# Four sums of z per chunk on GpSimd instead of two on VectorE, in the first stage of a three-part layer

## Chip, cores and metric

One Trainium2 chip, one core of it. The metric is the device time of the whole program in microseconds, the median of several executions. The engines are TensorE (matrix products), VectorE, ScalarE, GpSimd, and SyncE, which here only issues DMAs. Their names in the profile: PE is TensorE, PEld its weight loads, DVE VectorE, ACT ScalarE, POOL GpSimd, SP SyncE.

## The reference

```python
# first stage: for 64 rows (batch), T = 128 tokens, N = 64 complex states, L = 1024
Wc = Wc * num * _reciprocal(den * Lam, EPS)
P = dt_Lambda[..., None] * pos - P_max[..., None]
K = jnp.einsum('chn,hnl->chl', Wc, jnp.exp(P))
h = K.real                                  # (64, 128, 1024)
# then, per batch row:
h = h + attention(layernorm(h), Wq, Wk, Wv, Wo)   # 32 heads, 8 kv heads, rope, causal
h = h + ffn(layernorm(h), A, B, Wr, br)           # 8 softly mixed low-rank experts
```

For each token the first stage is a product of a 64 x 128 matrix (real and imaginary parts of the weights) by a 128 x 1024 matrix of complex powers. Only this stage is touched by the change.

## The kernel before, in words

`s4_stage` is the first stage, `layer_stage` (attention and feed-forward, 64 batch rows one after the other) the second. The second starts when all blocks of the first are through.

**Factored powers.** The 1024 positions of a token are taken apart into 4 parts of 256 (`TOPS`), and each part into 16 x 16 (`DIG`, `SEG`). The tile `z` of a *pair* of tokens holds, per token, two halves (s = 0 and 1) of 256 columns: the products of 16 digits by 16 steps. The factor of the part goes into the other operand, `xw`, which is the weight of the token times the power of its part, in real and imaginary form. The matmuls of a token are `hps += xw x z`, once for each half of z, for two column ranges of `hps`. If the two halves are added beforehand (the *sum* of this text), one matmul of a kind does for two. In the profile a matmul of f32 counts as two instructions, so a pair has 16 instructions in L612 without the sum and 8 with it.

**Loops.** 128 tokens are 64 pairs g; a *window* w has 4 tokens (2 pairs), a *chunk* k has 16 tokens, which is 4 windows or 8 pairs; there are 32 windows and 8 chunks. Pair 8k is the first of chunk k. `summed(g)` says which pairs are summed: before, pairs 3 and 7 of each chunk, and all eight pairs of the last chunk.

**The order on each engine**, written out by hand in one program each; they meet only at semaphores:

- VectorE, per window w: `swapped(w + 1)` (L467, L473: writes `pi`, the swapped part of the products, and the fourth token of `xw`; each reads one input from SBUF and one from PSUM), `table_z` for the two pairs (L487; `u` in PSUM, `tab` in SBUF), then the sums (L494; both inputs in `z`, SBUF) if there are any, then an extra step: in the first window of a chunk `angles(k + 1)` (L425 to L435), in the third `tables(k + 1)` (L441, L445), in the fourth `digits(k + 1)` (L454 to L458). At the end of windows 4k+1, 4k+2, 4k+3 comes `weight_lo` (L499) for a piece of the second stage's weights: `wq_lo`, `wo_lo`, `wkv_lo`; `aw_lo` and `bm_lo` come once, in windows 4 and 8. `angles`, `tables`, `digits` and `weight_lo` have all their inputs in SBUF. `table_z(g)` waits for the matmuls of pair g - 4 (four buffers of z), `swapped(w + 1)` for `add(w)`.
- ScalarE, per window w: in the second window of a chunk first the three sines (L351 to L354); then for each of the 4 tokens the products of window w + 3 (L364, four instructions, for 3 of the 4 tokens) and `evict` (L374, the copy of `hps` to `hout`, after the token's matmuls); at the end `weight_hi` (L379) for the piece whose `weight_lo` VectorE has in window w + 1. `weight_lo` waits for it.
- GpSimd, per window w: in windows 4k+1, 4k+3 and 4k+4 first a step of the tables of chunk k+1: `first_angles` (L255), `table_i` (L259), `digits_m1` (L262), each behind a wait for the `weight_lo` that VectorE has in the window before (`w_lo`); then `add(w)` (L322, `xw += pi`), which waits for `swapped(w)`.
- TensorE, per window: waits for `add(w)` (`xw_done`), per pair for `table_z` (`z_made`) and, if the pair is summed, for its sum (`z_sum`); then the matmuls (L612) of the two tokens, each of which waits until `hps` has been copied four tokens earlier.
- SyncE loads `x` and the weights and stores each pair's `hout`.

The condition and the sum as they stand:

```python
def summed(g):
    return g // (TC // 2) == CHUNKS - 1 or g % 2 == 1 and g // 2 % PER_CHUNK in SUM_AT   # SUM_AT = (1, 3)

def sum_z(g):                                                                            # VectorE
    zg = z[g % ZR][:, :, :].rearrange("p (t s) l -> p t s l", s=2)
    dve.wait_ge(z_made, g + 1)
    V.tensor_tensor(zg[:, :, 0, :], zg[:, :, 0, :], zg[:, :, 1, :], ALU.add).then_inc(z_sum, 1)
```

Of the kernel before, what the change touches and what calls it, by code (L numbers as in the profile page):

```python
# [15 lines left out]
ALU = mybir.AluOpType  # L16
# [5 lines left out]
T = 128  # L22
# [24 lines left out]
TC = 16  # L47
CHUNKS = T // TC
WIN = 4
WINDOWS = T // WIN  # L50
PER_CHUNK = TC // WIN
XT = 8
ZR = 4
# [75 lines left out]
def s4_stage(nc, x, log_dt, lam, wq, wk, wv, wo, aw, bm, br, consts, h0, W):  # L129
# [4 lines left out]
    with ExitStack() as ctx:  # L134
        def sb(name, shape, dt=f32):
            return ctx.enter_context(nc.sbuf_tensor(name, shape, dt))

        def sem(name):
            return ctx.enter_context(nc.semaphore(name))
# [7 lines left out]
        z = [sb(f"z{i}", [P, 4, QROW]) for i in range(ZR)]  # L147
# [68 lines left out]
        z_made = sem("z_made")  # L216
        z_sum = sem("z_sum")
# [2 lines left out]
        h_sent = [sem(f"h_sent{i}") for i in range(HR)]  # L220

        TV, TA, TP = 10, 3, 3
        SUM_AT = (1, 3)

        def summed(g):
            return g // (TC // 2) == CHUNKS - 1 or g % 2 == 1 and g // 2 % PER_CHUNK in SUM_AT

        def sums_before(g):
            return sum(summed(n) for n in range(g))
# [24 lines left out]
        def first_angles(eng, k):  # L254
            return eng.tensor_tensor(theta[:, :, :], across(zi, k, NPOS),  # L255
                                     pos[:, :].unsqueeze(1).broadcast_to([P, TC, NPOS]), ALU.mult)

        def table_i(eng, k):
            return eng.tensor_tensor(tab[k % 2][:, :, 1, :], expo[:, k * TC:k * TC + TC, :], theta[:, :, :], ALU.mult)  # L259

        def digits_m1(eng, k):
            return eng.tensor_tensor(dm1[:, :, :].rearrange("p t (s n) -> p t s n", s=2), across(rr, k, 2, DIG),  # L262
                                     tab[k % 2][:, :, :, 0:DIG], ALU.mult)

        with nc.Block() as block:
# [50 lines left out]
            @block.gpsimd  # L316
            def _(pool):
                def add(w):
                    pool.wait_ge(pr_done, w + 1)
                    pool.wait_ge(pi_done, w + 1)  # L320
                    xw_w = xw[w % XWR]
                    nc.gpsimd.tensor_tensor(xw_w[:, :, :, :], xw_w[:, :, :, :], pi[:, :, :, :],  # L322
                                            ALU.add).then_inc(xw_done, 1)

                pool.wait_ge(pre_v, N_PRE)
                for w in range(WINDOWS):
                    k, at = (w - 1) // PER_CHUNK, (w - 1) % PER_CHUNK
                    if w >= 1 and k + 1 < CHUNKS:
                        lows = sum(piece[0] < w - 1 for piece in PIECES)
                        if at in (0, 2, 3) and lows:  # L330
                            pool.wait_ge(w_lo, lows)
                        if at == 0:
                            pool.wait_ge(tab_v, TV * k + 10)
                            first_angles(nc.gpsimd, k + 1).then_inc(tab_p, 1)
                        if at == 2:
                            pool.wait_ge(tab_a, TA * (k + 1) + 2)
                            pool.wait_ge(z_made, k * (TC // 2))
                            table_i(nc.gpsimd, k + 1).then_inc(tab_p, 1)
                        if at == 3:
                            pool.wait_ge(tab_v, TV * (k + 1) + 7)  # L340
                            pool.wait_ge(tab_p, TP * (k + 1) + 2)
                            digits_m1(nc.gpsimd, k + 1).then_inc(tab_p, 1)
                    add(w)

            @block.scalar
            def _(act):
# [29 lines left out]
                def weight_hi(n):  # L376
                    _, name, k, width, _ = PIECES[n]
                    act.wait_ge(w_in[n % 2], loads_until(n))
                    A.activation(weight(name + "_hi", k), wst[n % 2][:, 0:width], ACT.Copy, scale=WS).then_inc(w_hi, 1)  # L379
# [30 lines left out]
            def _(dve):  # L410
                V = nc.vector
# [26 lines left out]
                def tables(k):  # L438
                    dve.wait_ge(tab_a, TA * k + 3)
                    dve.wait_ge(pre_a, 7 if k else 6)  # L440
                    V.tensor_scalar(half[:, :, :], half[:, :, :], -2.0, 1.0, ALU.mult, ALU.add).then_inc(tab_v, 1)  # L441
                    if k == 0:
                        table_i(V, k).then_inc(tab_p, 1)
                    dve.wait_ge(tab_v, TV * k + 6)
                    V.tensor_tensor(tab[k % 2][:, :, 0, :], expo[:, k * TC:k * TC + TC, :], half[:, :, :],  # L445
                                    ALU.mult).then_inc(tab_v, 1)
# [14 lines left out]
                def swapped(w):  # L461
                    q, slot = w // 2, w // 2 % XR
                    dve.wait_ge(x_in[slot], 48 * (q // XR + 1))
                    if w >= 1:
                        dve.wait_ge(xw_done, w)
                    t = WIN * w
                    V.tensor_tensor(pi[:, :, :, :],  # L467
                                    xb[slot][:, t % XT:t % XT + WIN, :].unsqueeze(2).broadcast_to([P, WIN, TOPS, NB]),
                                    top_i3[:, t:t + WIN, :].unsqueeze(3).broadcast_to([P, WIN, TOPS, NB]), ALU.mult)
                    if w >= XWR:  # L470
                        dve.wait_ge(tok_done, WIN * (w - XWR) + WIN)
                    rest, n = slice(t % XT + ON_ACT, t % XT + WIN), WIN - ON_ACT
                    V.tensor_tensor(xw[w % XWR][:, ON_ACT:, :, :],  # L473
                                    xa[slot][:, rest, :].unsqueeze(2).broadcast_to([P, n, TOPS, NB]),
                                    top_p3[:, t + ON_ACT:t + WIN, :].unsqueeze(3).broadcast_to([P, n, TOPS, NB]),
                                    ALU.mult).then_inc(pi_done, 1)

                def table_z(g):
                    k, at = g // (TC // 2), g % (TC // 2)
                    if g >= ZR:  # L480
                        dve.wait_ge(tok_done, 2 * (g - ZR) + 2)
                    if at == 0:
                        dve.wait_ge(tab_v, TV * k + 10)
                        dve.wait_ge(tab_p, TP * k + 2)
                    digit = u[k % 2][:, :].rearrange("p (s n) -> p s n", n=DIG)[:, 4 * at:4 * at + 4, :]
                    step_ = tab[k % 2][:, 2 * at:2 * at + 2, :, DIG:].rearrange("p t s n -> p (t s) n")
                    V.tensor_tensor(z[g % ZR][:, :, :].rearrange("p s (a b) -> p s a b", a=DIG),  # L487
                                    digit.unsqueeze(3).broadcast_to([P, 4, DIG, SEG]),
                                    step_.unsqueeze(2).broadcast_to([P, 4, DIG, SEG]), ALU.mult).then_inc(z_made, 1)

                def sum_z(g):
                    zg = z[g % ZR][:, :, :].rearrange("p (t s) l -> p t s l", s=2)
                    dve.wait_ge(z_made, g + 1)
                    V.tensor_tensor(zg[:, :, 0, :], zg[:, :, 0, :], zg[:, :, 1, :], ALU.add).then_inc(z_sum, 1)  # L494

                def weight_lo(n):
                    _, name, k, width, _ = PIECES[n]
                    dve.wait_ge(w_hi, n + 1)
                    V.scalar_tensor_tensor(weight(name + "_lo", k), wst[n % 2][:, 0:width], WS,  # L499
                                           weight(name + "_hi", k), ALU.mult, ALU.subtract).then_inc(w_lo, 1)  # L500
# [75 lines left out]
                for w in range(WINDOWS):  # L576
                    k, at = w // PER_CHUNK, w % PER_CHUNK
                    if 0 < w < WINDOWS - 1:
                        swapped(w + 1)
                    for g in (2 * w, 2 * w + 1):  # L580
                        table_z(g)
                    if w == 0:
                        swapped(1)
                    for g in (2 * w, 2 * w + 1):
                        if summed(g):
                            sum_z(g)
                    if k + 1 < CHUNKS:
                        if at == 0:
                            angles(k + 1)
                        if at == 2:  # L590
                            tables(k + 1)
                        if at == 3:
                            digits(k + 1)
                    for n, piece in enumerate(PIECES):
                        if piece[0] == w:
                            weight_lo(n)
# [885 lines left out]
```

## Time and profile before

| | |
|---|---|
| median of 3 runs | 2400.07 us (2398.28 to 2400.16) |
| the profiled execution | 2402.11 us |
| its span, first to last instruction | 2400.3 us |
| busy share, TensorE | 95% (2279.7 us) |
| VectorE | 79% (1906.4 us) |
| ScalarE | 77% (1838.1 us) |
| GpSimd | 71% (1709.9 us) |
| mean granted clock of TensorE | 0.985 |
| first stage | to about 260 us of the span |

The shares are means over both stages. The second stage is nine tenths of the span, so they describe it; the first has to be read in its own stretches. A granted clock of 1.00 is 2.4 GHz, 0.50 is 1.2 GHz. The 1.7 us between the span and the execution's time lie around the first and the last instruction.

### The profile page before, as it was taken

What the parts mean: (1) busy time and instruction counts of PE and PEld (TensorE: products, weight loads), DVE (VectorE), ACT (ScalarE), POOL (GpSimd) and SP (SyncE); (2) the same over time, 40 slices, a digit from 0 to 9 for tenths busy, and PEclk for the clock granted to TensorE, in tenths of its full rate; (3) what the DMA queues carried; (4) which work ended last, traced back from release to release, by engine and by line L of the source; (5) the groups of instructions that cost most, each with busy time, mean ns of one, the idle gap of its engine ahead of it and who ended that gap; (6) DMA issues with size and microseconds to landing.
All of it is one profiled execution on the core that took longest, in us unless ns stands there. A gap on an engine that the chain in (4) does not pass through costs nothing.

```text
span 2400.3 us, 58812 instructions
## 1 busy us (share of the span) xinstructions
PE 2279.7 (95%) x18704; PEld 1248.2 (52%) x18704; DVE 1906.4 (79%) x7796; ACT 1838.1 (77%) x6270; POOL 1709.9 (71%) x1529
## 2 busy tenths in 40 slices
PE   2999599999999999999999999999999999999986
PEld 2777345555555555555555555555555555555543
DVE  8999467888788888887887888788788878878864
ACT  5998378877777787877778787777877777787773
POOL 1444078777777777777777777777777777777782
PEclk9999799999999999999999999999999999999998
DMA  2888479999999999999999999999999999999985
GB/s 76 259 251 240 118 152 181 189 185 191 190 189 184 192 190 185 188 190 189 186 192 191 184 187 193 186 186 192 191 189 184 190 190 183 192 191 190 182 169 107
DMA packets 1201574, 443.65 MB, mean 185 GB/s; under 512 B 1151600, under 2 KB 1153904, under 8 KB 1201264
## 3 DMA queue, kind: packets, MB, share of 16 engines
q1 hardware_dynamic: 1201264, 439.89, 91.9%
q8 instruction: 149, 2.44, 0.4%
q14 instruction: 161, 1.32, 0.2%
HBM read 87.42 MB, written 67.11 MB: 64 GB/s over the span
## 4 chain that ended last, share of the span: by engine, by line
PE 85%; DMA 1%; DVE 1%; ACT 1%; POOL 0%; issue 0%; SPq 0%; POOLq 0%; ACTq 0%; DVEq 0%
PE pb L876 14%; PE pa L876 14%; PE pc L876 13%; PE s_ps L889 5%; PE pa L862 5%; PE pb L862 5%; PE pb L864 5%; PE pb L863 5%; PE pa L863 5%; PE pa L864 5%; PE pv_ps L904 4%; PE pd L862 1%; PE pd L864 1%; PE pd L863 1%; DMA pt<-p 1%; PE pd L962 1%
## 5 line engine op out<-in xcount | busy, mean ns | idle before, releaser
L1024 ACT ACTIVATE pr<-pr,smin 128x128 f32<-128x128 f32 x2048 | 793.5, 388 | 234.3 <-DVE smin L1165 234.1
L1372 POOL TENSOR_TENSOR pr<-pr,rinv 128x512 f32<-128x512 f32 x512 | 577.7, 1138 | 424.1 <-DVE rinv L1173 413.0
L1165 DVE CUSTOM_DVE_ANT_0 pr<-s_ps,cst 128x128 f32<-128x128 f32 x2048 | 468.6, 286 | 181.8 <-PE s_ps L889 101.4
L1380 POOL TENSOR_TENSOR p<-pr,p 128x512 f16<-128x512 f32 x512 | 590.7, 1159 | 24.6 <-ACT p L1034 14.0
L1034 ACT ACTIVATE p<-pr 128x512 f16<-128x512 f32 x512 | 319.0, 623 | 184.1 <-POOL pr L1372 154.2
L1024 ACT ACTIVATION_READ_ACCUMULATOR pr<-pr,smin 128x1 f32 x2048 | 382.3, 187 | 0.0
L876 PE MATMUL pa<-wkv_hi,xt 128*128 128x512 f16 x1024 | 327.0, 381 | 23.9 <-DMA xt<-xs 23.9
L876 PE MATMUL pb<-wq_hi,xt 128*128 128x512 f16 x1024 | 327.9, 381 | 0.0
L876 PE MATMUL pc<-wq_hi,xt 128*128 128x512 f16 x1024 | 315.0, 379 | 0.0
L612 PE MATMUL hps<-z,xw 128*128 128x256 f32 x848 | 195.5, 391 | 62.1 <-POOL xw L322 42.1
L612 PEld LDWEIGHTS hps<-z,xw 128*128 128x128 f32 x848 | 164.2, 196 | 93.1 <-POOL xw L322 50.3
L889 PE MATMUL s_ps<-kt,qt 128*128 128x128 f16 x2048 | 199.2, 220 | 7.8 <-issue 4.0
L889 PEld LDWEIGHTS s_ps<-kt,qt 128*128 128x128 f16 x2048 | 149.6, 98 | 105.8 <-DVE smin L1165 4.7
L876 PE MATMUL pb<-wq_lo,xt 128*128 128x512 f16 x512 | 196.3, 383 | 0.0
L876 PE MATMUL pa<-wkv_lo,xt 128*128 128x512 f16 x512 | 196.0, 383 | 0.0
L862 PE MATMUL pa<-wo_hi,ctx_t 128*128 128x512 f16 x512 | 195.1, 381 | 0.2 <-DVE ctx_t L1179 0.2
L863 PE MATMUL pa<-wo_lo,ctx_t 128*128 128x512 f16 x512 | 195.0, 381 | 0.0
L864 PE MATMUL pa<-wo_hi,ctx_t 128*128 128x512 f16 x512 | 194.7, 380 | 0.0
L863 PE MATMUL pb<-wo_lo,ctx_t 128*128 128x512 f16 x512 | 194.6, 380 | 0.0
L864 PE MATMUL pb<-wo_hi,ctx_t 128*128 128x512 f16 x512 | 194.6, 380 | 0.0
L862 PE MATMUL pb<-wo_hi,ctx_t 128*128 128x512 f16 x512 | 194.5, 380 | 0.0
L876 PE MATMUL pc<-wq_lo,xt 128*128 128x512 f16 x512 | 194.0, 379 | 0.0
(186 smaller groups left out, 4893.0 us busy)
## 6 DMA issues: line engine op xcount, KB each, us to landing
h<-hout SPq DMA_DIRECT2D x128, 256.0 KB, 3.5
h_ln<-h SPq DMA_DIRECT2D x64, 512.0 KB, 4.4
h_res<-h SPq DMA_DIRECT2D x64, 512.0 KB, 4.6
out<-h SPq DMA_DIRECT2D x64, 512.0 KB, 3.2
pt<-p SPq DMA_TRANSPOSE x512, 3.9
xa<-x SPq DMA_DIRECT2D x16, 256.0 KB, 4.0
xb<-x SPq DMA_DIRECT2D x32, 128.0 KB, 3.9
wst<-wq SPq DMA_DIRECT2D x8, 512.0 KB, 5.6
```

The source lines that it names most:

```text
L612: last = pe.matmul(hps[t % 4][:, QROW * i:QROW * i + QROW], xw[w % XWR][:, t % WIN, 2 * i:2 * i + 2, :], z[g % ZR][:, 2 * (t % 2) + m, :], ...
L862: pe.matmul(bank, x[:, k, :], w_hi[:, k, cols], start=(k == 0), stop=False)
L863: pe.matmul(bank, x[:, k, :], w_lo[:, k, cols], start=False, stop=False)
L864: last = pe.matmul(bank, x[:, KC + k, :], w_hi[:, k, cols], start=False, stop=(k == KC - 1))
L876: last = pe.matmul(bank, x[:, k if n < 2 * KC else KC + k, :], w[:, k, cols], start=(n == 0), stop=(n == 3 * KC - 1))
L889: last = pe.matmul(s_ps[g % 2][:, j * P:(j + 1) * P], qt[:, HG * g + j, :], kt[:, g, :], start=True, stop=True)
L904: last = pe.matmul(pv_ps[j * HD:(j + 1) * HD, to], v[:, g * HD:(g + 1) * HD], pt[g % RP][:, lo + j, :], start=(n == 0), stop=(n == 2))
L1024: last = A.activation(p, p, ACT.Exp, bias=smin[g % 2][:, j:j + 1], scale=-1.0, accum_out=rsum[g % 2][:, j:j + 1])
L1034: A.activation(p16[g % 2][:, 0:HG * P], pr[g % 2][:, :], ACT.Copy).then_inc(ph_done, 1)
L1165: V.tensor_tensor_reduce(pr[g % 2][:, cols], s_ps[g % 2][:, cols], mask, 1.0, 3e38, ALU.add, ALU.min, smin[g % 2][:, j:j + 1]).then_inc(ma ...
L1372: nc.gpsimd.tensor_tensor(p3, p3, rinv[g % 2][:, :].unsqueeze(2).broadcast_to([P, HG, P]), ALU.mult).then_inc(p_norm, 1)
L1380: nc.gpsimd.tensor_tensor(p[:, HG * P:], pr[g % 2][:, :], p[:, 0:HG * P], ALU.subtract).then_inc(pl_done, 1)
```

## The change

The sums move from VectorE's queue to GpSimd's. On GpSimd the sums of window w - 1 stand behind `add(w)`; those of the last window stand at the end, without an `add` ahead. Pairs 1, 3, 5 and 7 of each chunk are summed instead of pairs 3 and 7; in the last chunk all eight are, as before. TensorE's program is the same text, but follows `summed`.

```diff
-        SUM_AT = (1, 3)
+        SUM_AT = (1, 3, 5, 7)
 
         def summed(g):
-            return g // (TC // 2) == CHUNKS - 1 or g % 2 == 1 and g // 2 % PER_CHUNK in SUM_AT
+            return g // (TC // 2) == CHUNKS - 1 or g % (TC // 2) in SUM_AT
+
+        def sum_z(eng, g):
+            zg = z[g % ZR][:, :, :].rearrange("p (t s) l -> p t s l", s=2)
+            return eng.tensor_tensor(zg[:, :, 0, :], zg[:, :, 0, :], zg[:, :, 1, :], ALU.add)
...
                     add(w)
+                    for g in (2 * w - 2, 2 * w - 1):
+                        if w and summed(g):
+                            pool.wait_ge(z_made, g + 1)
+                            sum_z(nc.gpsimd, g).then_inc(z_sum, 1)
+                for g in (T // 2 - 2, T // 2 - 1):
+                    pool.wait_ge(z_made, g + 1)
+                    sum_z(nc.gpsimd, g).then_inc(z_sum, 1)
...
-                def sum_z(g):
-                    zg = z[g % ZR][:, :, :].rearrange("p (t s) l -> p t s l", s=2)
-                    dve.wait_ge(z_made, g + 1)
-                    V.tensor_tensor(zg[:, :, 0, :], zg[:, :, 0, :], zg[:, :, 1, :], ALU.add).then_inc(z_sum, 1)
...
-                    for g in (2 * w, 2 * w + 1):
-                        if summed(g):
-                            sum_z(g)
```

## Rows read from the trace of the kernel before

**Rows 1.** Table by stretches: length, then busy time and count per engine, clock, DMA

```profile
123.67:150.30 26.63, 25.10 (x114) 21.22 (x113) 24.82 (x33) 23.99 (x73) 12.84 (x7) 1.00 0.82 246
97.04:123.67 26.63, 24.94 (x114) 21.07 (x113) 25.87 (x34) 24.86 (x73) 12.86 (x7) 1.00 0.88 267
246.10:252.93 6.83, 4.81 (x11) 3.87 (x12) 6.83 (x8) 1.19 (x2) 1.22 (x1) 0.50 0.45 151
```

**Rows 2.** Timeline of VectorE, chunk 3, last one of chunk 1: start, us, what, idle before

```profile
123.67 1.22 DVE L467 TENSOR_TENSOR pi<-xb,top_i 128x1024 f32<-128x1024 f32 x1
...
127.39 0.61 DVE L425 TENSOR_SCALAR turns<-theta 128x512 f32<-128x512 f32 x1
128.04 0.43 DVE L427 TENSOR_SCALAR turns<-turns 128x512 f32<-128x512 f32 x1
...
134.14 0.76 DVE L494 TENSOR_TENSOR z<-z 128x512 f32<-128x512 f32 x1
135.20 1.23 DVE L499 SCALAR_TENSOR_TENSOR wq_lo<-wst,wq_hi 128x1024 f16<-128x1024 f32 x1 [0.30 <-ACT wq_hi L379]
...
142.64 1.23 DVE L499 SCALAR_TENSOR_TENSOR wo_lo<-wst,wo_hi 128x1024 f16<-128x1024 f32 x1 [1.23 <-ACT wo_hi L379]
...
150.30 1.22 DVE L467 TENSOR_TENSOR pi<-xb,top_i 128x1024 f32<-128x1024 f32 x1
...
77.02 1.28 DVE L499 SCALAR_TENSOR_TENSOR aw_lo<-wst,aw_hi 128x1088 f16<-128x1088 f32 x1
```

**Rows 3.** Timeline of TensorE, start of chunk 3

```profile
126.45 12.32 PE L612 MATMUL hps<-z,xw 128*128 128x256 f32 x56 [0.89 <-issue]
```

**Rows 4.** Timeline of ScalarE, chunk 3

```profile
133.63 0.60 ACT L374 ACTIVATE hout<-hps 128x512 f32<-128x512 f32 x1 [1.13 <-PE hps L612]
...
138.21 1.05 ACT L364 ACTIVATE xw<-xa,top_r 128x64 f32<-128x64 f32 x4
139.17 0.58 ACT L374 ACTIVATE hout<-hps 128x512 f32<-128x512 f32 x1
...
141.55 1.05 ACT L379 ACTIVATE wo_hi<-wst 128x1024 f16<-128x1024 f32 x1
```

**Rows 5.** Timeline of GpSimd, chunk 3

```profile
125.36 2.36 POOL L322 TENSOR_TENSOR xw<-xw,pi 128x1024 f32<-128x1024 f32 x1 [0.47 <-DVE xw L473]
...
136.51 1.28 POOL L259 TENSOR_TENSOR tab<-expo,theta 128x512 f32<-128x512 f32 x1 [2.16 <-DVE wq_lo L499]
```

**Rows 6.** Instructions of three lines: ns shortest/median/longest, first and last start

```profile
L1391 POOL TENSOR_TENSOR qr<-rt_c,rt_s x128: 1257/1269/1642, 292.8 to 2323.8; 128x512 f32<-128x512 f32 x128
L494 DVE TENSOR_TENSOR z<-z x22: 674/760/866, 52.2 to 252.4; 128x512 f32<-128x512 f32 x22
L441 DVE TENSOR_SCALAR turns<-turns x8: 428/610/1700, 34.3 to 220.0; 128x512 f32<-128x512 f32 x8
```

**Rows 7.** Timelines of VectorE and GpSimd, three places where they meet

```profile
44.12 2.45 DVE L427 TENSOR_SCALAR turns<-turns 128x512 f32<-128x512 f32 x1
43.89 2.39 POOL L322 TENSOR_TENSOR xw<-xw,pi 128x1024 f32<-128x1024 f32 x1 [0.79 <-DVE xw L473]
...
292.60 2.35 DVE L1221 TENSOR_TENSOR xs<-h_ln,xs 128x512 f16<-128x512 f32 x2
292.77 1.64 POOL L1391 TENSOR_TENSOR qr<-rt_c,rt_s 128x512 f32<-128x512 f32 x1 [0.77 <-DVE rt_s L1233]
...
342.82 0.80 DVE L1221 TENSOR_TENSOR xs<-h_ln,xs 128x512 f16<-128x512 f32 x1
340.65 2.42 POOL L1380 TENSOR_TENSOR p<-pr,p 128x512 f16<-128x512 f32 x2
343.03 1.18 POOL L1407 TENSOR_TENSOR kr<-kt_c,kt_s 128x256 f32<-128x256 f32 x1
```

**Rows 8.** Timeline of TensorE, last chunk

```profile
235.15 8.83 PE L612 MATMUL hps<-z,xw 128*128 128x256 f32 x32 [3.26 <-DVE z L494]
248.12 9.52 PE L612 MATMUL hps<-z,xw 128*128 128x256 f32 x32 [4.14 <-DVE z L494]
```

## The prediction, made before the changed kernel was run

> **What bounds the kernel now.** The busy shares (the table above) give TensorE 95% of the span, but that is the attention stage, which the change doesn't touch. The first stage (up to 260 us) has to be read by itself. In the table by stretches one chunk in its steady state takes 26.63 us [rows 1], and there VectorE has 24.82 us of work, ScalarE 23.99, TensorE 25.10 (its modelled ends overlap) and GpSimd 12.84. Three engines are nearly full, so the timelines of that chunk decide; it starts at 123.67 with `swapped` and the next one at 150.30.
>
> The order in VectorE's queue is `swapped`, two `table_z`, then the extras [rows 2]. Two pauses and two instructions matter: `wq_lo` waits 0.30 us and `wo_lo` 1.23 us for ScalarE's `_hi` conversions, and the two sums take 0.76 us each. Behind `wo_hi` stands this chain: TensorE starts pair 8k at 126.45, as soon as its z is there [rows 3], runs two unsummed pairs of 16 matmuls at about 0.215 us each, ScalarE waits 1.13 us for the fourth token's matmuls and copies it at 133.63, then come `wq_hi`, the sines and a window of products and copies without any pause, and `wo_hi` runs from 141.55 to 142.60 [rows 4]. So the chunk's loop is z(8k), TensorE, ScalarE, `wo_lo`, VectorE. TensorE's speed counts only in pair 8k+1; anything saved in VectorE ahead of `wo_lo` vanishes in the 1.23 us.
>
> **What the change removes.** (a) Pairs 8k+1 and 8k+5 fall from 16 to 8 matmuls. For 8k+5 nobody waits. For 8k+1 ScalarE would have its fourth token 1.7 us earlier. But the second token's copy stays at 130.2 (16 matmuls and 0.3 us after 126.45), and a copy, products and a copy (0.48, 0.96, 0.48 us from start to start [rows 4]) put the fourth at 132.10: 1.53 us are left. (b) VectorE loses two sums. One stands before `wo_lo` and is hidden, the other gives 0.79 us (0.76 and a gap of 0.03). If nothing else changed, the chunk would fall by 1.53 + 0.79 = 2.32 us to 24.3.
>
> **What it adds.** Four sums per chunk in GpSimd's queue, each behind the `add` of the next window and ahead of that engine's next table step and `add`. *Length:* no row shows this sum on GpSimd. The nearest is the addition of two full 128x512 f32 tiles, 1.27 us [rows 6]; the `add` of twice the size takes 2.36 us [rows 5], half of it 1.18. I take 1.27, and 1.18 to 1.35 as ends. The Trainium skill (GPSIMD Engine Reference, section Performance versus the Vector engine) has a two-input f32 operation 1.96 times slower on GpSimd than on VectorE; with VectorE's shortest sum, 0.67 us [rows 6], that is an estimate of 1.32 us, and the total below would be 1 us more. GpSimd's time is not the trouble: 12.84 + 4 x 1.27 = 17.9 us of 26.6.
>
> *The hold:* the trace shows that some VectorE instructions and GpSimd's don't run together [rows 7]. `turns` (L427, 0.43 us alone) was issued at 44.12 while an `add` ran from 43.89 to 46.28, and ended at 46.57, 0.29 us after it. It goes the other way too: GpSimd's `qr`, issued at 292.77 in the middle of VectorE's first `xs`, took 1.64 us for 1.27, and the second `xs` had to wait for it, so that the two took 2.35 us instead of 1.3. Whoever waits gets in when the other finishes: with two GpSimd instructions back to back (340.65 to 343.07, then 343.03), VectorE's `xs` of 342.82 went between them and GpSimd's second, half the size of `qr`, took 1.18 us, nearly as much as it. The instructions of VectorE that are held are those with two inputs in SBUF or one f32 input and output there: all of `angles`, `tables`, `digits`, `weight_lo`. `swapped` and `table_z` read one input from PSUM and ran beside every `add` unhindered. The kernel before keeps clear of this: GpSimd waits for `w_lo` ahead of its table steps, and only tails of 0.18 us are lost at L425 and L441 (0.61 for 0.43 us) [rows 2, 6].
>
> Now each new sum, by its place. A held VectorE instruction ends 0.14 us less than its length after GpSimd's; a held sum ends 1.12 us (1.27 - 0.15) after VectorE's.
> - Sum 8k+1 comes behind the `add` that ends at 127.72. L425 is already waiting, gets in and ends at 128.00; the sum holds until 129.12; L427 ends at 129.41 instead of 128.47: **+0.94**.
> - Sum 8k+3: `add` ends 0.3 us into `wq_lo`, which is held for **+0.18**; the sum follows until 1.12 us after it. Then `table_i` (1.28) and `add` (2.36) come 0.6 us later than VectorE would let them, and L441 waits for that `add`: 1.31 us instead of 0.43, **+0.88** (0.18 of it before already).
> - Sum 8k+5 gets in behind L441, and L445 waits: 1.12 + 0.55 instead of 0.69 us, **+0.95**.
> - Sum 8k+7: L454 is held by the `add`'s tail, **+0.19**; the sum gets in behind it, and L457 waits: **+0.95**.
> With L425's 0.18 that is 4.27 us a chunk. VectorE without waits, sums and holds needs 26.63 - 1.69 (the two waits and 0.08 of overlap lost at each) - 1.59 - 0.36 = 23.0 us. So the chunk becomes 23.0 + 4.27 = **27.3 us, 0.64 more than before**, bound by VectorE alone. ScalarE's `wo_hi` is ready more than 1 us before `wo_lo` asks, so the shorter pair 8k+1 buys nothing.
>
> **The sum.** Chunks 1 to 6: 6 x 0.64 = +3.8 us. `aw_lo` (1.28 us [rows 2]) and `bm_lo` stand in windows 4 and 8; before, VectorE's waits hid them (the chunk with `bm_lo` also takes 26.63 us [rows 1]); with no waits left they cost their lengths less the 0.08 us by which neighbours overlap, 1.20 and, with `wq_lo`'s length, 1.15: +2.3. Chunk 0 lies between -2.3 (all gain) and +0.6 (all hold): in its first half TensorE and a late `wo_hi` decide, as in the 24.3 us case, in its second the holds, as in the other; I take -1.2, a little to the side of the gain. Chunk 7 (all pairs summed before and after; 4.94 and 17.92 us after its start TensorE began pairs 56 and 60 [rows 8]): `add` of window 29 runs from 1.69 to 4.06 after the chunk's start, as `add` does in every chunk, sum 56 behind it to 5.3, so that pair 56 starts 0.5 us later than it did, and with it `wq_hi`, `wq_lo` and the last `swapped` (now 13.6). Its z are ready at 17.4, its `add` ends at 17.6, `wo_lo` waits for that and ends at 18.7, sum 60 is held by it until 19.8, and TensorE starts pair 60 at 20.1 instead of 17.92. From there it is as before: TensorE starts both its runs of 32 matmuls at the lower clock after idling 3.26 and 4.14 us [rows 8] (granted 0.50 in the stretch from 246.10 [rows 1]), and will again. +2.2. Total -1.2 + 3.8 + 2.3 + 2.2 = **+7.1 us**: the profiled execution of 2402.1 us becomes 2409.2, the median of the runs shown, 2400.1, becomes **2407.2**. The attention stage only starts later; where its first matmuls fall against the clock's changes can move it by 2 us either way.
>
> **Rivals.** *GpSimd's sums hide (faster).* Were the sums to meet none of VectorE's held instructions, the chunk would take 24.3 us, 7 x -2.32 = -16.2, with chunk 7's +2.2: 2386. It decides from where the holds fall under 26.63 - 23.0 = 3.6 us a chunk. The long quiet stretches of GpSimd speak for it, the rows of the hold against: 8%.
> *Half a hold (faster or same).* If instructions with two SBUF inputs were held less than the f32 `turns` ones, L445, L457 and the short tails would drop out: 27.3 - 1.9 - 0.4 = 25.0 us a chunk, 7 x -1.6 and the +2.3 and +2.2: 2393. The `xs` at 292.60 has two SBUF inputs and was held in full [rows 7], so I give it 6%. [...] One hold less than I count (a sum that slips in beside a `table_z`) is 6.5 us less: 2400.7, no change; with smaller slips, 24%.
> *The clock falls inside the chunks (slower still).* TensorE now idles some 2.4 us before pairs 8k+2 and 8k+6, where 0.89 us went by before pair 8k [rows 3]; the clock fell after 3.26 us [rows 8]. The slack ahead of `wo_lo` takes up most of a fall, but up to 0.5 us a chunk may come through: 2411. It shares in the 62% of slower.
> That GpSimd is late for TensorE doesn't happen: each sum is ready before its pair's predecessor is through, or 0.1 us after.
>
> **Chances.** A measurement of this kernel tells 0.2%, 4.8 us, from no change. Forecast with the clock rival 62% (slower), no change 24%, faster 14%. The range runs from 2398 (two smaller holds, a short sum, no delay in chunk 7) to 2413 (sum 1.35 us long, clock falls, a late phase of the attention stage); it leaves out the two faster cases and the far tail.
>
> **What would show it.** Right: the chunk's period at 27.3 us; L427, L445, L457 at 1.3 to 1.7 us; no idle time of VectorE before `wo_lo`; GpSimd's sums at 1.27 us, held ones longer; ScalarE and TensorE with more idle time, L612 with 736 matmuls for 848 (7 x (4 x 16 + 4 x 8) + 64). Wrong: a period under 26.6 us, L427 at 0.43 us, VectorE waiting for `wo_hi` again.

## The result, and the profile after

The changed kernel takes 2408.72 us (median of 5 runs, 2408.29 to 2410.48) against 2400.07 us (5 runs, 2398.28 to 2402.85): a ratio of 1.0038 with a 95% interval of 1.0027 to 1.005. It is slower by 8.7 us, well outside the noise; 7.1 were forecast, and the forecast range of 2398 to 2413 holds it. The profiled execution took 2408.72 us, with a span of 2406.9.

The page gives the busy time of each engine over the whole span, first of the kernel before, then of the changed one:

```profile
PE 2279.7 (95%) x18704; PEld 1248.2 (52%) x18704; DVE 1906.4 (79%) x7796; ACT 1838.1 (77%) x6270; POOL 1709.9 (71%) x1529
PE 2264.4 (94%) x18592; PEld 1233.7 (51%) x18592; DVE 1918.4 (80%) x7774; ACT 1838.9 (76%) x6270; POOL 1766.8 (73%) x1565
```

VectorE has 22 instructions fewer and is busy 12 us *longer*. The missing work has turned into time in which its instructions stand still. TensorE has 112 matmul instructions fewer, GpSimd 36 more.

The table by stretches, as in [rows 1]: chunk 5, chunk 2 (with `bm_lo`), and a piece inside chunk 5. Behind the length stand busy time and count of PE, PEld, DVE, ACT and POOL, then the granted clock, the DMA share and GB/s.

```profile
181.09:208.37 27.28, 23.12 (x98) 19.17 (x97) 27.07 (x31) 23.79 (x71) 19.47 (x11) 0.94 0.81 241
97.75:126.18 28.43, 23.13 (x98) 19.18 (x97) 28.22 (x31) 24.75 (x72) 19.47 (x11) 0.94 0.80 230
191.60:195.00 3.40, 3.40 (x9) 2.69 (x9) 3.40 (x4) 2.11 (x6) 3.40 (x3) 0.50 0.87 262
```

A chunk takes 27.28 us for 26.63, and VectorE is busy for 27.07 of them where it was for 24.82. Here are its rows in chunk 5, which answer to [rows 2]; below them GpSimd's, then one of TensorE and two of ScalarE (timeline: start, us, engine, line, idle time before). In this kernel L436, L438, L452, L456, L465, L468, L505 are the L425, L427, L441, L445, L454, L457, L499 of before, L478 and L484 are `swapped`, L326 is `add`, L263 `table_i`, L615 the matmuls, L385 the copy, L390 `weight_hi`, and L230 is the sum. In the experiments all of these shift by a few lines; the names of the tiles stay.

```profile
181.09 1.21 DVE L478 TENSOR_TENSOR pi<-xb,top_i 128x1024 f32<-128x1024 f32 x1
...
184.82 0.60 DVE L436 TENSOR_SCALAR turns<-theta 128x512 f32<-128x512 f32 x1
185.45 1.38 DVE L438 TENSOR_SCALAR turns<-turns 128x512 f32<-128x512 f32 x1
...
192.38 1.41 DVE L505 SCALAR_TENSOR_TENSOR wq_lo<-wst,wq_hi 128x1024 f16<-128x1024 f32 x1
...
197.44 1.32 DVE L452 TENSOR_SCALAR turns<-turns 128x512 f32<-128x512 f32 x1
198.79 1.65 DVE L456 TENSOR_TENSOR tab<-expo,turns 128x512 f32<-128x512 f32 x1
200.37 1.21 DVE L505 SCALAR_TENSOR_TENSOR wo_lo<-wst,wo_hi 128x1024 f16<-128x1024 f32 x1
...
205.23 0.86 DVE L465 TENSOR_TENSOR turns<-ss,tab 128x512 f32<-128x512 f32 x1
206.13 1.39 DVE L468 TENSOR_TENSOR u<-theta,turns 128x256 f32<-128x256 f32 x1
...
208.37 1.21 DVE L478 TENSOR_TENSOR pi<-xb,top_i 128x1024 f32<-128x1024 f32 x1
...
182.77 2.36 POOL L326 TENSOR_TENSOR xw<-xw,pi 128x1024 f32<-128x1024 f32 x1 [0.48 <-DVE xw L484]
185.08 1.46 POOL L230 TENSOR_TENSOR z<-z 128x512 f32<-128x512 f32 x1
190.34 2.37 POOL L326 TENSOR_TENSOR xw<-xw,pi 128x1024 f32<-128x1024 f32 x1 [3.80 <-DVE xw L484]
192.67 2.25 POOL L230 TENSOR_TENSOR z<-z 128x512 f32<-128x512 f32 x1
194.88 1.27 POOL L263 TENSOR_TENSOR tab<-expo,theta 128x512 f32<-128x512 f32 x1
196.11 2.36 POOL L326 TENSOR_TENSOR xw<-xw,pi 128x1024 f32<-128x1024 f32 x1
198.43 1.47 POOL L230 TENSOR_TENSOR z<-z 128x512 f32<-128x512 f32 x1
...
205.51 1.72 POOL L230 TENSOR_TENSOR z<-z 128x512 f32<-128x512 f32 x1
...
191.43 12.29 PE L615 MATMUL hps<-z,xw 128*128 128x256 f32 x48 [2.16 <-issue]
...
195.07 0.60 ACT L385 ACTIVATE hout<-hps 128x512 f32<-128x512 f32 x1 [1.37 <-PE hps L615]
199.25 1.06 ACT L390 ACTIVATE wo_hi<-wst 128x1024 f16<-128x1024 f32 x1
```

Read the VectorE and GpSimd rows against each other. L438 was issued at 185.45 and its own length is 0.43 us; GpSimd's sum runs to 186.54, and L438 ends at 186.83, 0.29 us later. GpSimd's sum of 192.67 lasts 2.25 us because `wq_lo`, itself held by `add`, runs until 193.79; the sum ends 1.13 us after it. `table_i` and `add` follow, to 198.47, and L452 of 197.44 ends at 198.76, again 0.29 us later. Then the next sum, and L456 waits for that. Nothing in VectorE's rows says "idle": the held time is inside the instructions.

### The profile page after: what moved, and what is told of

It reads as the page before. It is cut to its first block, busy times and chain, and to the rows that moved or that the text cites. A ratio compares the mean times of both kernels' runs of the same rounds, so it can differ in the third digit from the quotient of the medians.

```text
span 2406.9 us, 58603 instructions
## 1 busy us (share of the span) xinstructions
PE 2264.4 (94%) x18592; PEld 1233.7 (51%) x18592; DVE 1918.4 (80%) x7774; ACT 1838.9 (76%) x6270; POOL 1766.8 (73%) x1565
## 3 DMA queue, kind: packets, MB, share of 16 engines
q14 instruction: 161, 1.32, 0.2%
## 4 chain that ended last, share of the span: by engine, by line
PE 85%; DMA 1%; DVE 1%; ACT 1%; POOL 0%; issue 0%; SPq 0%; POOLq 0%; DVEq 0%; ACTq 0%
PE pb L879 14%; PE pa L879 14%; PE pc L879 13%; PE s_ps L892 5%; PE pa L865 5%; PE pa L866 5%; PE pa L867 5%; PE pb L865 5%; PE pb L867 5%; PE pb L866 5%; PE pv_ps L907 4%; PE pd L865 2%; PE pd L867 1%; PE pd L866 1%; PE pd L965 1%; PE pd L967 1%
## 5 line engine op out<-in xcount | busy, mean ns | idle before, releaser
L615 PE MATMUL hps<-z,xw 128*128 128x256 f32 x736 | 181.6, 410 | 83.7 <-POOL xw L326 42.1
L615 PEld LDWEIGHTS hps<-z,xw 128*128 128x128 f32 x736 | 149.9, 206 | 115.1 <-issue 50.0
```

Of the source, the lines that this page charges most:

```text
L615: last = pe.matmul(hps[t % 4][:, QROW * i:QROW * i + QROW], xw[w % XWR][:, t % WIN, 2 * i:2 * i + 2, :], z[g % ZR][:, 2 * (t % 2) + m, :], ...
```

## The experiments

The theory is the **hold**: a VectorE instruction with all its data in SBUF and a GpSimd instruction exclude each other, and each sum on GpSimd costs VectorE what it takes there. Against it stand the number and place of the sums, fixed costs of queues and semaphores, and TensorE or the memory traffic as bound. All ratios are against the kernel before, run on the same chip; "chunk" is the distance from one chunk's `swapped` to the next one's, in chunks 4 to 6.

**e1: four sums, but on VectorE.** The kernel before with

```diff
-        SUM_AT = (1, 3)
+        SUM_AT = (1, 3, 5, 7)
...
-            return g // (TC // 2) == CHUNKS - 1 or g % 2 == 1 and g // 2 % PER_CHUNK in SUM_AT
+            return g // (TC // 2) == CHUNKS - 1 or g % (TC // 2) in SUM_AT
```

> The four sums of a chunk stay on VectorE, in the place of the kernel before (pairs 1, 3, 5, 7). Theory of the hold: GpSimd has no sums, so L427, L445 and L457 take their own 0.43, 0.69 and 0.43 us; VectorE has 23.0 us and four sums at 0.80 (0.73 and the tail of an add), so a chunk of 26.2 us, and with aw_lo and bm_lo uncovered (chunks 1 and 2 at 27.4) the whole is about as the kernel before: 2399 us, 2396 to 2402. Rival (the engine of the sums does not matter, their number and place do, four of them cost what two saved in TensorE): as the changed kernel, 27.3 us a chunk and 2408 us.

Measured: 2399.43 us, ratio 1.0 (0.9991 to 1.001); chunk 26.13 us; chunks 1 and 2 at 27.67 and 27.46. The timeline of VectorE in chunk 5 and at the start of the next:

```profile
175.80 1.21 DVE L467 TENSOR_TENSOR pi<-xb,top_i 128x1024 f32<-128x1024 f32 x1
...
180.77 0.43 DVE L427 TENSOR_SCALAR turns<-turns 128x512 f32<-128x512 f32 x1
...
193.66 0.69 DVE L445 TENSOR_TENSOR tab<-expo,turns 128x512 f32<-128x512 f32 x1
...
200.64 0.43 DVE L457 TENSOR_TENSOR u<-theta,turns 128x256 f32<-128x256 f32 x1
...
201.92 1.21 DVE L467 TENSOR_TENSOR pi<-xb,top_i 128x1024 f32<-128x1024 f32 x1
```

The same sums cost 1.15 us a chunk less where VectorE does all of them itself, and L427, L445 and L457 have their own lengths. So the whole loss of the change comes from the move to GpSimd. Four sums at 1, 3, 5, 7 against two at 3 and 7, all on VectorE, come out even in the total only: the steady chunk is 0.50 us shorter, but chunks 1 and 2, where `aw_lo` and `bm_lo` are no longer hidden, are 1.03 and 0.82 us longer.

**e2: two sums, but on GpSimd.** The changed kernel with

```diff
-        SUM_AT = (1, 3, 5, 7)
+        SUM_AT = (3, 7)
```

> Only the engine changes: pairs 3 and 7 are summed, as before, on GpSimd. Theory of the hold: sum 8k+3 falls on wq_lo and costs nothing, because wo_lo waits for ScalarE anyway (still about 1 us idle before it); sum 8k+7 falls on L457 (1.39 us instead of 0.43) and the tail of the add on L454 (0.87), in the place of a sum of 0.80 us on VectorE: a chunk of 27.0 us, chunk 7 2.4 us longer, total 2404 to 2406 us. Rival (VectorE gains what it no longer does): 26.63 - 0.80 = 25.8 us a chunk, 2395 us.

Measured: 2403.76 us, ratio 1.0016 (1.0007 to 1.0026), just under the 2404 expected; chunk 26.99 us, the expected 27.0.

```profile
189.49 1.47 DVE L505 SCALAR_TENSOR_TENSOR wq_lo<-wst,wq_hi 128x1024 f16<-128x1024 f32 x1 [1.10 <-ACT wq_hi L390]
...
196.92 1.23 DVE L505 SCALAR_TENSOR_TENSOR wo_lo<-wst,wo_hi 128x1024 f16<-128x1024 f32 x1 [0.98 <-ACT wo_hi L390]
...
202.70 1.39 DVE L468 TENSOR_TENSOR u<-theta,turns 128x256 f32<-128x256 f32 x1
```

The change of engine alone loses 4.0 us. What VectorE saves ahead of `wo_lo` turns into waits for ScalarE (1.10 and 0.98 us here, 0.30 and 1.23 before); the sum behind `wo_lo`, the only one that counted, comes back as 0.96 us in L468 and 0.20 in the instruction before it.

**e3: half the sum.** The changed kernel; in chunks 0 to 6 only 128 of the 256 columns of each token are added, so the rest of z lacks its second half.

```diff
-            return eng.tensor_tensor(zg[:, :, 0, :], zg[:, :, 0, :], zg[:, :, 1, :], ALU.add)
+            n = QROW if g // (TC // 2) == CHUNKS - 1 else 128
+            return eng.tensor_tensor(zg[:, :, 0, 0:n], zg[:, :, 0, 0:n], zg[:, :, 1, 0:n], ALU.add)
```

> The changed kernel with half the columns added in chunks 0 to 6 (128 of the 256 of each token; the other columns of z lack the second half). The sum then takes about 0.73 us on GpSimd for 1.27. Theory of the hold: each of the holds of L427, L441, L445, L457 falls by 0.54 us (to 0.84, 0.78, 1.10 and 0.85 us), so the chunk by 2.1 us to 25.1; total 2392 to 2396 us. Rival (the holds are a matter of queues or semaphores, a fixed cost per sum): L427, L445 and L457 stay at 1.37, 1.64 and 1.39 us and the chunk at 27.3.

Measured: 2397.71 us, ratio 0.9991 (0.9982 to 1.0); chunk 25.12 us. Timelines of VectorE and GpSimd:

```profile
178.41 0.83 DVE L439 TENSOR_SCALAR turns<-turns 128x512 f32<-128x512 f32 x1
...
189.87 0.79 DVE L453 TENSOR_SCALAR turns<-turns 128x512 f32<-128x512 f32 x1
190.69 1.10 DVE L457 TENSOR_TENSOR tab<-expo,turns 128x512 f32<-128x512 f32 x1
...
197.48 0.84 DVE L469 TENSOR_TENSOR u<-theta,turns 128x256 f32<-128x256 f32 x1
...
178.04 0.92 POOL L231 TENSOR_TENSOR z<-z 128x256 f32<-128x256 f32 x1
```

The four holds fell as stated (0.84, 0.78, 1.10, 0.85 expected), and the chunk by 2.16 us. The cost goes with the length of GpSimd's instructions, not with their number. The total is 2 us above the range that I expected: chunks 1 to 3 took 26.33, 27.33 and 26.53 us, where I had left `aw` and `bm` out of the estimate, and chunk 7, whose sums are whole, 31.18 us.

**e4: next to no sum.** As e3 with `2` for `128`: two columns in 256, in chunks 0 to 6.

> The changed kernel with 2 of 256 columns added in chunks 0 to 6: GpSimd's four instructions and their semaphores stay, the time they hold is nearly gone. Theory: no holds but the two tails of add; VectorE would need 23.4 us, ScalarE's chain z(8k), TensorE, evictions, wq_hi, sines, wo_hi, wo_lo sets the chunk at 24.3 to 24.6 us, VectorE waits some 0.9 us for wo_hi; total 2384 to 2388 us. Rival (DMA or something else holds the chunk near 26): no wait of VectorE for ScalarE, 26 us or more.

Measured: 2392.96 us, ratio 0.9972 (0.9962 to 0.9982); chunk 24.49 us, as expected, total 5 us above the range. Timeline of VectorE, chunks 3 and 5:

```profile
137.51 1.22 DVE L506 SCALAR_TENSOR_TENSOR wo_lo<-wst,wo_hi 128x1024 f16<-128x1024 f32 x1 [0.34 <-ACT wo_hi L391]
...
186.48 1.22 DVE L506 SCALAR_TENSOR_TENSOR wo_lo<-wst,wo_hi 128x1024 f16<-128x1024 f32 x1 [0.68 <-ACT wo_hi L391]
```

With the holds gone VectorE waits for `wo_hi` again, by 0.68 us in the steady chunks (0.9 expected): the loop through TensorE and ScalarE is the floor, 2.14 us a chunk under the kernel before. The 5 us are chunks 1 and 2 (26.28 and 25.99 us; ScalarE has `aw_hi` and `bm_hi` there, and VectorE `aw_lo` and `bm_lo`) and the long chunk 7, 29.85 us.

**e5: pairs 1 and 3 on VectorE.** The condition of e1 with

```diff
-        SUM_AT = (1, 3, 5, 7)
+        SUM_AT = (1, 3)
```

> The kernel before with pairs 1 and 3 of a chunk summed on VectorE instead of 3 and 7. Theory (the loop z(8k), TensorE, ScalarE, wo_lo, VectorE): the shorter pair 8k+1 takes 1.5 us out of ScalarE's chain, no sum is left behind wo_lo, so VectorE's own work binds: 23.0 + 2 x 0.8 + tails of add at L441 and L454 = 25.0 us a chunk, 26.2 in chunks 1 and 2 (aw_lo, bm_lo, aw_hi, bm_hi uncovered), chunk 7 unchanged; total 2389 to 2393 us. Rival (which pairs are summed is of no account, 16 and 8 matmuls come to the same 112 a chunk): 26.6 us a chunk and 2400 us.

Measured: 2391.43 us, ratio 0.9966 (0.9953 to 0.9978): **faster than both kernels**, with as many sums and matmuls as the kernel before. Chunk 25.5 to 25.7 us, not 25.0. The timelines of VectorE and TensorE, and the table by stretches for that chunk:

```profile
190.21 1.23 DVE L499 SCALAR_TENSOR_TENSOR wo_lo<-wst,wo_hi 128x1024 f16<-128x1024 f32 x1 [0.69 <-ACT wo_hi L379]
...
170.66 10.31 PE L612 MATMUL hps<-z,xw 128*128 128x256 f32 x47
181.57 5.42 PE L612 MATMUL hps<-z,xw 128*128 128x256 f32 x24 [0.60 <-issue]
187.23 12.97 PE L612 MATMUL hps<-z,xw 128*128 128x256 f32 x59 [0.24 <-issue]
```

```profile
171.57:197.27 25.70, 24.86 (x115) 21.22 (x114) 24.74 (x32) 23.99 (x72) 12.85 (x7) 1.00 0.85 255
```

The pairs 8k+4 to 8k+7 are now all unsummed, and behind them comes pair 8k: TensorE runs without a gap into the next chunk and starts pair 8k (the 24th matmul from the end of the first TensorE row, at 175.63) 1.4 us after its z is there, where it was 0.1 us before. `wo_lo` waits 0.69 us for what comes of it. I had left that out. That the total lies inside the expected range all the same is luck: chunk 7, which I expected unchanged, took 25.99 us for 28.07, and in this trace TensorE kept the higher clock (granted 1.00) all through it.

**e6: pairs 1 and 5 on VectorE.** As e5 with `SUM_AT = (1, 5)`.

> As before with pairs 1 and 5 on VectorE. Theory: window 4k+1 now has two unsummed pairs, so ScalarE gets its fourth token 1.7 us later than with pairs 1 and 3, wo_hi comes later and VectorE waits about 1 us for it again: 25.7 to 25.9 us a chunk, 2394 to 2397 us. Rival (VectorE's work alone counts): the same as with pairs 1 and 3, 24.8 us or less.

Measured: 2396.19 us, ratio 0.9985 (0.9975 to 0.9994); chunk 25.83 us. The same number of sums in two other places differs by 4.8 us. Its `wo_lo` waits 0.81 us for ScalarE.

**e7: one wait more.** The changed kernel; sum 8k+1 is kept until `angles` is through.

```diff
                             pool.wait_ge(z_made, g + 1)
+                            if g % (TC // 2) == 1 and g // (TC // 2) + 1 < CHUNKS:
+                                pool.wait_ge(tab_v, TV * (g // (TC // 2) + 1) + 5)
```

> The changed kernel, where GpSimd holds sum 8k+1 back until VectorE's angles are through, so that it runs beside swapped (one input in PSUM). One wait is added, no work. Theory of the hold: L427 falls from 1.37 to 0.43 us and the chunk by 0.94 to 26.3 us, though TensorE gets pair 8k+1 some 2.5 us later; total 2401 to 2403 us. Rival (a sum costs wherever it stands, or its lateness costs more): chunk at 27.3 us or above.

Measured: 2409.99 us, ratio 1.0047 (1.0032 to 1.0063): a miss. Chunk 27.25 us where 26.3 was expected. Timelines of VectorE and GpSimd:

```profile
159.73 0.43 DVE L440 TENSOR_SCALAR turns<-turns 128x512 f32<-128x512 f32 x1
...
167.17 1.22 DVE L507 SCALAR_TENSOR_TENSOR wq_lo<-wst,wq_hi 128x1024 f16<-128x1024 f32 x1 [1.37 <-ACT wq_hi L392]
...
172.68 1.64 DVE L458 TENSOR_TENSOR tab<-expo,turns 128x512 f32<-128x512 f32 x1
174.60 1.23 DVE L507 SCALAR_TENSOR_TENSOR wo_lo<-wst,wo_hi 128x1024 f16<-128x1024 f32 x1 [0.28 <-ACT wo_hi L392]
...
162.22 1.27 POOL L230 TENSOR_TENSOR z<-z 128x512 f32<-128x512 f32 x1 [2.80 <-DVE theta L448]
```

The hold is gone as the theory says: the sum runs 1.27 us beside `swapped`, L440 takes 0.43 us, and L454, no longer behind a late `add`, 0.60. But VectorE now stands for 1.37 us before `wq_lo` and 0.28 before `wo_lo`. Pair 8k+1 starts 1.93 us later in the chunk than in the changed kernel, and `wq_hi` ends 1.81 us later; `wq_lo` had only 1.33 us of room there, and VectorE, rid of the hold, is ready for it 0.86 us sooner. What the hold gave back became waits.

**e8: chunk 7 as before.** The changed kernel with the last chunk's eight sums on VectorE.

```diff
-                        if w and summed(g):
+                        if w and summed(g) and g // (TC // 2) < CHUNKS - 1:
...
+                    if k == CHUNKS - 1:
+                        for g in (2 * w, 2 * w + 1):
+                            dve.wait_ge(z_made, g + 1)
+                            dve.wait_ge(z_sum, sums_before(g - g % 2))
+                            sum_z(V, g).then_inc(z_sum, 1)
```

> The changed kernel with the eight sums of chunk 7 back on VectorE. Theory: chunks 0 to 6 as changed (27.3 us), chunk 7 back from 30.5 to 28.1 us: total 2406 to 2407 us. Rival (chunk 7 is longer because of the clock or of the stores, not of GpSimd): chunk 7 stays above 30 us and the total at 2409.

Measured: 2405.98 us, ratio 1.0029 (1.002 to 1.0038). Chunk 7 fell from 30.52 to 26.39 us (from its `swapped` to the end of the last copy), 1.7 more than expected; in this execution, one of the quicker ones (2404.82 us), TensorE kept the higher clock through the first half of the chunk. The medians differ by 2.7 us. In all the traces chunk 7 takes 26.0 to 28.1 us with its sums on VectorE and 29.6 to 31.2 with them on GpSimd, so they are a loss there, though the clock differs between these traces too.

## Why the prediction was right, point by point

| term | forecast | measured |
|---|---|---|
| chunk 4, 5, 6 | 27.27 us | 27.29, 27.28, 27.28 |
| chunk 3 | 27.27 | 27.62 |
| chunks 1, 2 (`aw`, `bm`) | +1.84, +1.79 | +1.86, +1.79 |
| chunk 0 | -1.2 | -1.13 |
| chunk 7 | +2.2 | +2.45 |
| all chunks, to the last copy | +7.1 | +7.9 |
| passage and attention stage | 0, 2 either way | +1.8 up to its first matmul, -3.0 from there on |

- **The hold** was read right from three meetings in the old trace [rows 7], and e3 and e7 confirm it. L438, L456 and L468 took 1.38, 1.65 and 1.39 us where 1.37, 1.64 and 1.38 were worked out, L452 1.32 for 1.31. The sum alone takes 1.27 us (1.267 at its shortest in the changed kernel), against the 1.27 taken from `qr`; the estimate of 1.32 from the Trainium skill's ratio for two-input operations (GPSIMD Engine Reference, section Performance versus the Vector engine) was 0.05 us high. The same page of the Trainium skill, section Specifications, says that GpSimd shares its SBUF interfaces with VectorE, with contention "with DVE instructions in a 2-port perf mode or with two SBUF inputs". The traces agree for the second kind, L456 and L468, held to 1.65 and 1.39 us for 0.69 and 0.43. For the first no trace names the mode; L438, which has one f32 input and takes 0.43 us alone for 512 columns where two inputs take 0.69, was held to 1.38. With L456 and L468 held in full the rival "half a hold" is out.
- **Who wins** was right too. VectorE's waiting instruction goes in at the end of `add` before the next sum (L436 at 0.60 us, `wq_lo` at 1.41), and the sum goes in before VectorE's next one.
- **What GpSimd's sums would have given** without the hold: 24.3 us a chunk was forecast, e4 has 24.49.
- **The slack of ScalarE** was right at the higher clock only. I wrote that `wo_hi` would be ready more than 1 us before `wo_lo` asks. In the row it ends at 200.31 and `wo_lo` starts at 200.37. Idle for 2.16 us before pair 8k+2 (2.4 forecast), TensorE ran at the lower clock from 191.60 to 195.00, and ScalarE waited 1.37 us for it. This is the rival of the clock: it came in this place in chunks 2 to 6, and of the 0.5 us a chunk that I feared nothing came through. e8, which is the same kernel up to chunk 6, shows the other case. In its chunk 5 the clock stayed up behind a gap of 2.18 us:

```profile
191.40 10.74 PE L617 MATMUL hps<-z,xw 128*128 128x256 f32 x48 [2.18 <-issue]
...
197.54 1.06 ACT L387 ACTIVATE wo_hi<-wst 128x1024 f16<-128x1024 f32 x1
...
200.34 1.21 DVE L502 SCALAR_TENSOR_TENSOR wo_lo<-wst,wo_hi 128x1024 f16<-128x1024 f32 x1
```

  The 48 matmuls take 10.74 us instead of 12.29, `wo_hi` is there 1.74 us before `wo_lo` starts, and the chunk takes 27.30 us all the same. So the slack is about 1.7 us, and a fall of 3.4 us at this place just fits into it, with 0.06 us left. I had worked out neither of the two; that nothing at all comes through is luck.
- **Chunk 0's** -1.2 was picked between two bounds, not worked out; that it was -1.13 is luck.
- **Chunk 3** has 0.34 us more than its neighbours: its first `add` starts 0.49 us after `swapped` instead of 0.15, which lengthens the hold of L436 to 0.94 us. The same `add` is late by as much in e3, e4 and e8, so it isn't chance, but it isn't in e1, e2 and e5 to e7. What delays it stays open.
- **Chunk 7**: TensorE started pair 56 at 241.17, 5.52 us after the chunk's start, and pair 60 at 256.60, after 20.95 us (20.1 forecast; 17.92 before). That the whole chunk is still near the forecast is partly luck: "from there it is as before" was wrong in both directions. TensorE's first run took 9.63 us for 8.83 before, because 5.0 us of it instead of 3.4 were at the lower clock; its last run took 8.75 for 9.52, with 3.3 us instead of 4.8.

```profile
241.17 9.63 PE L615 MATMUL hps<-z,xw 128*128 128x256 f32 x32 [4.19 <-POOL z L230]
256.60 8.75 PE L615 MATMUL hps<-z,xw 128*128 128x256 f32 x32 [5.80 <-DVE z L498]
```

- **The passage to the attention stage** adds 1.8 us, and the stage itself gives back 3.0, which is more than my 2 us. The last copy ends 7.9 us later than before (266.17 for 258.28), the first load of the next stage lands later still, and the first matmul there comes 9.65 us later (287.63 for 277.98). From the chain that ended last, the load in the kernel before, then the load and the first matmul in the changed one:

```profile
263.12 3.21 DMA h_ln<-h
...
271.12 4.90 DMA h_ln<-h
...
287.63 1.46 PE pa L879 x3
```

That load took 1.7 us longer; why stays open. From the first matmul to the end the stage then took 2119.3 us, where the profiled execution of before had 2122.3; the eight experiments have 2119.4 to 2121.1. That profiled execution, 2402.1 us, lies 2 us over its own median, so some of its 3 us are the execution and not the kernel. This is also why the two profiled executions differ by 6.6 us and the medians by 8.7.

## What to carry to other kernels

Before moving an elementwise operation to GpSimd, list which VectorE instructions will stand in the queue at that moment. In these traces those with two SBUF inputs, and those with one f32 input and the output in SBUF, stopped until GpSimd's instruction was through, and the lost time was shown as their busy time and not as idle. Those that read one of two inputs from PSUM ran on (`swapped` took 1.21 to 1.22 us with or without a sum beside it). And if two engines meet in a loop, choose the places of the work before its engine: moving two sums from pairs 3 and 7 to pairs 1 and 3, on the same engine, gave 8.4 us (e5), where moving the same two sums to the other engine lost 4.0 (e2).

## What the runs showed of the hardware beyond what was expected

- The exclusion is complete and orderly in the trace of the changed kernel. L438, held by a sum in every chunk (f32, one input, 512 columns), ended 0.28 to 0.29 us after it, L456 (two inputs, 512 columns) 0.55 us, and a held sum 1.12 to 1.14 us after VectorE's instruction; when both wait, they take turns.
- TensorE's clock fell from 2.4 to 1.2 GHz (granted 1.00 to 0.50) after gaps of 2.16 us in the changed kernel's chunks, as in the stretch from 191.60 to 195.00; the trace of before showed it in the first stage only after 3.26 and 4.14 us. But the length of the gap alone doesn't tell: in e8 it stayed up after 2.18 us before 191.40 and fell after 2.12 us before 176.94, and in the changed kernel it stayed up after 3.35 us before 80.80. After the gaps of 1.45 us it always stayed. The mean granted clock of chunks 2 to 6 was 0.94, and VectorE, which sets their length, shows no wait for it.
- `aw_lo` and `bm_lo` cost nothing while VectorE waited for ScalarE, and 1.20 and 1.15 us, their lengths less the overlap, once it didn't (chunks 1 and 2 took 1.86 and 1.79 us more than before, of which 0.65 is the change in every chunk).
